# Fused adaLN block: the row of negated maxima written by eight one-column DMAs instead of a TensorE transposition, a ScalarE copy and one DMA

## What is computed

```
mod = (silu(c) @ wmod).reshape(16, 6, 1, 256)          # sa, ca, ga, sb, cb, gb; ga and gb floored at 0.25
h = layernorm(x) * (1 + ca) + sa
q = h @ Wq.T;  kv = h @ Wkv_down.T;  k = kv @ Wk_up.T;  v = kv @ Wv_up.T     # 8 heads of 64
attn = softmax(q k^T / 8)
x = x + ga * ((attn @ v) @ Wo.T)
h = layernorm(x) * (1 + cb) + sb
x = x + gb * (h @ weight.T + pooled(h) @ disha)
```

## Time and profile before

| | |
|---|---|
| median of 3 runs | 3070.46 us (3069.53 to 3070.96) |
| profiled execution | 3068.32 us, of which the span of instructions 3065.3 us |
| granted TensorE clock, mean | 0.996 of full speed |
| busy: PE / DVE / ACT / POOL | 98% / 70% / 56% / 83% |
| chain that ended last | PE 94%, DVE 2%, POOL 2%, DMA 1%, ACT 1% |
| DMA packets | 165621, 162.93 MB |

### The profile page before, as it was taken

How to read it: one execution, slowest core, us unless ns; L and a number is a source line. 1 busy time by engine, 2 the same in 40 slices (tenths; PEclk the granted TensorE clock), 3 DMA queues, 4 the chain that set the end, 5 groups by cost and what they waited for, 6 DMA issues and landing times.

```text
span 3065.3 us, 45400 instructions
## 1 busy us (share of the span) xinstructions
PE 3014.4 (98%) x15394; PEld 1696.1 (55%) x15394; DVE 2146.2 (70%) x2548; ACT 1720.2 (56%) x3209; POOL 2544.3 (83%) x1520
## 2 busy tenths in 40 slices
PE   6999999999999999999999999999999999999998
PEld 4445555555555555555555555555555555555545
DVE  5466767767677676777767677676776767667665
ACT  3555555555555555555555555555555555555544
POOL 2788888888888888888888888888888888888796
PEclk9999999999999999999999999999999999999999
DMA  3111121121111111121211211211121111111111
GB/s 86 39 52 44 51 62 53 50 59 53 53 47 59 56 49 53 56 60 46 60 46 53 63 50 50 61 52 53 49 64 49 49 54 55 60 39 53 46 48 47
DMA packets 165621, 162.93 MB, mean 53 GB/s; under 512 B 62224, under 2 KB 113552, under 8 KB 165392
## 3 DMA queue, kind: packets, MB, share of 16 engines
q1 hardware_dynamic: 165392, 160.05, 17.8%
HBM read 74.40 MB, written 17.33 MB: 30 GB/s over the span
## 4 chain that ended last, share of the span: by engine, by line
PE 94%; DVE 2%; POOL 2%; DMA 1%; ACT 1%; issue 1%; SPq 0%; ACTq 0%; DVEq 0%; POOLq 0%
PE ps_mix L647 29%; PE ps_score L668 18%; PE ps_score L670 15%; PE ps_max L696 11%; PE ps_side L633 7%; PE ps_side L762 5%; PE ps_side L781 3%; PE ps_side L748 2%; POOL prob_sum L1043 1%; PE ps_side L714 1%; PE ps_side L738 1%; PE ps_side L769 1%; ACT probs L872 1%; DMA query_m<-max_row 0%; DVE neg_max L1197 0%
## 5 line engine op out<-in xcount | busy, mean ns | idle before, releaser
L1043 POOL TENSOR_TENSOR prob_sum<-prob_sum,probs 128x1024 f32<-128x1024 f32 x768 | 1861.1, 2423 | 352.8 <-ACT probs L872 275.8
L1197 DVE TENSOR_REDUCE neg_max<-ps_max 128x1 f32<-128x1024 f32 x1024 | 1204.3, 1218 | 310.9 <-PE ps_max L696 306.9
L872 ACT ACTIVATE probs<-ps_score 128x512 f32<-128x512 f32 x2048 | 1113.3, 597 | 474.0 <-PE ps_score L670 448.8
L647 PE MATMUL ps_mix<-probs,values 128*64 128x512 f32 x4096 | 935.4, 598 | 0.8 <-ACT probs L872 0.8
L668 PE MATMUL ps_score<-query,key_hi 128*128 128x512 f32 x2048 | 881.0, 430 | 9.4 <-ACT probs L872 7.9
L670 PE MATMUL ps_score<-query_m,key_lo 128*128 128x512 f32 x2048 | 809.5, 395 | 0.0
L647 PEld LDWEIGHTS ps_mix<-probs,values 128*64 128x64 f32 x4096 | 271.3, 136 | 532.8 <-issue 531.6
L668 PEld LDWEIGHTS ps_score<-query,key_hi 128*128 128x128 f32 x2048 | 384.7, 188 | 260.5 <-ACT probs L872 100.8
L670 PEld LDWEIGHTS ps_score<-query_m,key_lo 128*128 128x128 f32 x2048 | 386.7, 189 | 45.2
L696 PE MATMUL ps_max<-key_hi,query 64*128 64x512 f32 x2048 | 376.2, 445 | 3.7 <-DVE neg_max L1197 3.7
L1043 POOL TENSOR_TENSOR prob_sum<-probs 128x1024 f32<-128x1024 f32 x128 | 311.6, 2434 | 56.4 <-ACT probs L872 56.4
(11 more groups left out here) (203 smaller groups left out, 2860.0 us busy)
## 6 DMA issues: line engine op xcount, KB each, us to landing
query_m<-query SPq DMA_DIRECT2D x128, 256.0 KB, 2.5
query_m<-query SPq DMA_DIRECT2D x256, 128.0 KB, 2.6
recip<-recip_scratch SPq DMA_DIRECT2D x254, 128.0 KB, 2.9
x_in<-in_L_attn_x_dram SPq DMA_DIRECT2D x32, 512.0 KB, 4.8
x_mid<-in_L_attn_x_dram SPq DMA_DIRECT2D x64, 256.0 KB, 3.2
out_dram<-x_mid SPq DMA_DIRECT2D x64, 256.0 KB, 2.2
denoms<-recip SPq DMA_DIRECT2D x508, 1.0 KB, 1.7
gates<-gates_scratch SPq DMA_DIRECT2D x16, 256.0 KB, 4.5
```

The source lines that it names most:

```text
L647: last = nc.tensor.matmul(ps_mix[j * R:j * R + R, :], values[par][:, k, :], probs[:, (STEPS * z.c + s) % RING, j * HALF:(j + 1) * HALF], s ...
L872: nc.scalar.activation(probs[:, (STEPS * z.c + s) % RING, half * HALF:(half + 1) * HALF], ps_score[half], ACT.Exp, scale=SCALE).then_inc(e ...
L1043: nc.gpsimd.tensor_tensor(out=total[:, :], in0=before, in1=probs[:, now % RING, :], op=ALU.add).then_inc(adds_done, 1)
L1197: nc.vector.tensor_reduce(neg_max[:, col:col + 1], ps_max[j][:, :], AX_X, ALU.max, negate=True).then_inc(maxima_done, 1)
```

## The change

Step 5 loses the transposition on PE and the copy on ACT. SP issues, at step 5 instead of step 6, eight DMAs, each from one column of `neg_max` (128 partitions, one element each) to 128 neighbouring elements of row 127 of `query_m`. It waits for the maxima themselves. `neg_max` is declared F32R, as `max_row` was. The counts of `max_row_set` become eight times as large. Nothing else of the order changes, except that "max_row" is no piece of the side bank any more.

```diff
-    "max_row": (60,) + tuple(STEPS - NT + 5 + NT * i for i in range(1, GROUPS)),
...
-        neg_max = sb("neg_max", [P, STEPS])
-        max_row = [sb(f"max_row{i}", [NT, P], F32R) for i in range(2)]
+        neg_max = sb("neg_max", [P, STEPS], F32R)
...
-                        copy, row = STEPS + NT * (j - 1) + 1, step_of("max_row", j) + 1
+                        copy, row = STEPS + NT * (j - 1) + 1, STEPS + NT * (j - 1) + 5
...
-                            drained(sp, z, "max_row", j, need_alone)
+                            need_alone(sp, maxima_done, STEPS * b + NT * (j + 1))
                             need_alone(sp, query_m_copied, 48 * (GROUPS * b + j + 1))
 
-                            need_alone(sp, max_row_set, 16 * (GROUPS * b + j))
-                            sp.dma_start(query_m[P - 1:P, j % 2, :].bitcast(F32),
-                                         max_row[j % 2][:, :].bitcast(F32)).then_inc(max_row_set, 16)
+                            need_alone(sp, max_row_set, 16 * NT * (GROUPS * b + j))
+                            for u in range(NT):
+                                sp.dma_start(query_m[P - 1:P, j % 2, u * P:(u + 1) * P].bitcast(F32),
+                                             neg_max[:, NT * j + u:NT * j + u + 1].bitcast(F32),
+                                             allow_slow_non_contiguous=True).then_inc(max_row_set, 16)
...
-                        need(pe, max_row_set, 16 * (GROUPS * z.c + g + 1))
+                        need(pe, max_row_set, 16 * NT * (GROUPS * z.c + g + 1))
...
-                    elif kind == "max_row":
-                        need(pe, maxima_done, STEPS * b + NT * (i + 1))
-                        need(pe, side_drained[room], count)
-                        last = nc.tensor.transpose(side[0:NT, 0:P], neg_max[:, NT * i:NT * (i + 1)], ident[:, :])
...
-                        elif kind == "max_row":
-                            need(act, side_full[room], count + 1)
-
-                            need(act, max_row_set, 16 * (GROUPS * b + i - 1))
-                            nc.scalar.activation(max_row[i % 2][:, :], side[0:NT, 0:P], ACT.Copy).then_inc(side_drained[room], 1)
```

More of the change, by code:

```diff
@@ L103, in step_of @@
     return {
-        "max_row": STEPS - NT + 5 + NT * i,
         "denominator": NT * (i + 1) + 1,
@@ L135 @@
 FOLDS = {"wo_t": (2, 1), "gate": (1, 1), "mod_out": (1, 1), "wo_fold": (4, 1), "weight_t": (2, 1)}
-PIECES = {"norm_t": (2 * NF, 1), "latent": (2, 1), "values_t": (2, 1), "query": (2 * PAIRS, 1), "max_row": (GROUPS, 1),
+PIECES = {"norm_t": (2 * NF, 1), "latent": (2, 1), "values_t": (2, 1), "query": (2 * PAIRS, 1),
           "denominator": (GROUPS, 0), "out_proj": (NT, -1), "norm2_t": (CHUNKS, -1), "ffn": (CHUNKS, -1)}
```

## The result

The changed kernel takes 3257.39 us (median of 6 runs, 3250.74 to 3267.13) against 3070.56 for the kernel before, a ratio of 1.061 (95% interval 1.0598 to 1.0621). The forecast was 3143, so 72 us of loss were expected and 187 came. The direction and the place are as forecast. The size is not.

A forecast was written before the change was run, and what follows sets the result against it. PE, 94% of the chain that ended last, was taken as the bound. Profiled 3068.3 + 74 for late rows - 2 for the removed transposition = 3140; with the runs' median 2.1 us above the profiled one, forecast 3143 us, range 3090 to 3270.

The forecast's parts named there:

- The direction and the place: At PE's step 0, the wait for the row: slower, 73 of 128 groups late, 74 us more in all.
- 0.62 and 0.76 us, 74 or 193 us in all: SP's issue pitch per column: forecast took 0.63 us, 74 us in all; heavier issues 0.76, 193 us, chance 0.20.
- landing: On SP's burst, from the last column's issue to its arrival: 1.7 us, then 0.05 us until PE starts.

## What to carry to other kernels

Replacing one transfer by n on the queue that carries a dependent chain costs n - 1 pitches between the producer and the reader, and the pitch can be bounded from the trace before by the nearest transfers with the same memories on both sides. Here these gave 0.62 and 0.76 us, 74 or 193 us in all, and only the run told which. When the working puts many groups within a few tenths of a microsecond of the limit, give the small terms (landing, an occasional slow landing) their spread. And when a change makes an otherwise busy TensorE stall for more than a microsecond, ask what the clock does after the stall, since whatever is tied to its steps will be late once more.

## What was not expected of the hardware

- A burst of eight transfers of 512 bytes inside SBUF issues at 0.62 to 0.63 us each whether the pieces are 128 of 4 bytes or 16 of 32; the pieces show in the landing (2.04 against 1.70 us).
- With one-element transfers issued 0.1 to 0.2 us behind a 128 KB broadcast on the same queue it lands some 0.6 us later (3.54 against 2.95), with such transfers from two queues 1.5 us later (4.46). Where a load stands between and they start 0.7 to 0.8 us behind, the delay is under 0.2 (3.09 to 3.13). Transfers with larger pieces were not tried in that place.
- In the changed kernel half of the stalls of 1.5 us and more were followed by a stretch at half clock that cost 1.5 us, and none of the shorter ones.
- A 4 KB store that lands in 1.4 us took about 3.1 to 3.2 us on the mean in the groups where it overlapped a 16 KB packet of the instruction queue, and which groups these were followed PE's program, not the length of the groups.
